# Attention over heads in blocks of two tokens instead of four, in a fused decoder layer on one NeuronCore

## The reference

```python
# 1 attention: over the 16 HEADS of one token, not over tokens
q, k, v = rope(x @ wq.T), rope(x @ wk.T), x @ wv.T      # each (b, s, 16 heads, 16)
weights = softmax(einsum('bshd,bstd->bsht', q, k) / 4)   # per token a 16 by 16 matrix
x = layernorm(x + einsum('bsht,bstd->bshd', weights, v).reshape(b, s, 256) @ wo.T)
# 2 WKV: recurrence over the 128 tokens with k = x, v = ctx
x = layernorm(x + wkv(time_decay, time_first, x, ctx))
# 3 FFN with quantised activations (8 bit, by the row's maximum) and ternary weights
h = silu(bitlinear(x, w1)) * bitlinear(x, w2)            # 704 wide
x = layernorm(x + bitlinear(h, w3))
```

## Time and profile before

| | us |
|---|---|
| median of 3 runs (lowest, highest) | 262.02 (260.38, 263.08) |
| the profiled execution | 262.2 |
| its span, first to last instruction | 260.4 |
| PE busy | 208.2 (80%) |
| DVE busy | 217.7 (84%) |
| ACT busy | 160.9 (62%) |
| POOL busy | 161.5 (62%) |

### The profile page before, as it was taken

The page is one execution under the profiler, slowest core; times in us unless marked ns, Lnnn a source line. Parts: engine busy times, 40 slices in busy tenths (PEclk is TensorE's granted clock), DMA queues, the critical chain, the costliest instruction groups (busy, mean ns, idle before and its releaser), DMA issues.

```text
span 260.4 us, 9989 instructions
## 1 busy us (share of the span) xinstructions
PE 208.2 (80%) x3778; PEld 139.9 (54%) x3778; DVE 217.7 (84%) x544; ACT 160.9 (62%) x329; POOL 161.5 (62%) x336
## 2 busy tenths in 40 slices
PE   1759699989899999999999999999997795625611
PEld 0235457657666666666666666766665662413310
DVE  2534987999999999999999999999999977686331
ACT  2212175446686877777777787777777665655631
POOL 0100007647866869696968778787777787876541
PEclk9986869999999999999999999999999757555665
DMA  6920002102020020212201120203020201000001
GB/s 194 369 66 23 3 1 65 58 7 64 4 64 3 3 83 23 65 29 58 61 26 43 44 71 17 84 3 83 5 63 3 63 3 40 10 13 21 0 20 42
DMA packets 11968, 12.34 MB, mean 47 GB/s; under 512 B 1872, under 2 KB 11152, under 8 KB 11920
## 3 DMA queue, kind: packets, MB, share of 16 engines
q1 hardware_dynamic: 11200, 11.67, 14.5%
q10 hardware_dynamic: 720, 0.03, 0.2%
HBM read 9.60 MB, written 2.10 MB: 45 GB/s over the span
## 4 chain that ended last, share of the span: by engine, by line
PE 50%; DVE 22%; issue 18%; ACT 4%; POOL 3%; DMA 1%; DVEq 1%; POOLq 0%; ACTq 0%
PE ps_qkv L393 13%; PE ps_s L429 9%; PE ps_o L476 5%; PE ps_w L379 4%; DVE amax_h L972 4%; PE ps_c L528 4%; DVE vT L863 3%; PE ps_a L514 3%; DVE qkD L858 3%; PE ps_b L514 3%; DVE gate L965 2%; DVE den_rec L941 2%; PE ps_o L379 2%; DVE wsum L1009 2%; PE ps_o L462 2%
## 5 line engine op out<-in xcount | busy, mean ns | idle before, releaser
L393 PE MATMUL ps_qkv<-wqkv,xT 128*128 128x512 f32 x64 | 35.5, 683 | 1.9 <-DVE qkv_tok L842 1.9
L733 POOL TENSOR_TENSOR var_eps<-mv,eps 128x1 f32<-128x1 f32 x48 | 9.2, 192 | 39.8 <-DVE mv L925 39.3
L745 POOL TENSOR_TENSOR hid<-gate,up_s 128x352 f32<-128x352 f32 x32 | 29.8, 932 | 2.1 <-ACT up_s L628 1.8
L736 POOL TENSOR_TENSOR rstd<-var_eps,minus_half 128x1 f32<-128x1 f32 x48 | 26.4, 551 | 3.8
L941 DVE RECIPROCAL den_rec<-frac 128x256 f32<-128x256 f32 x16 | 27.7, 1733 | 0.0
L429 PE MATMUL ps_s<-qkD 20*64 20x64 f32 x1024 | 23.9, 234 | 3.3 <-PE ps_s L429 3.3
L462 PE MATMUL ps_o<-probs,v_blk 64*32 64x64 f32 x1024 | 21.7, 225 | 4.6 <-DVE res L908 3.6
L577 ACT ACTIVATE qkv_tok<-ps_qkv 128x512 f32<-128x512 f32 x16 | 9.6, 598 | 25.3 <-PE ps_qkv L393 25.3
L387 PE MATMUL ps_qkv<-wqkv,xT 128*128 128x256 f32 x64 | 19.8, 431 | 6.1 <-DMA wqkv<-wqkv_in 5.3
L429 PEld LDWEIGHTS ps_s<-qkD 20*64 20x64 f32 x1024 | 19.8, 143 | 8.1 <-PE ps_s L429 5.1
L660 ACT ACTIVATE hqT<-ps_c 128x768 bf16<-128x768 bf16 x16 | 13.0, 811 | 16.4 <-PE ps_c L521 16.4
(11 more groups left out here) (110 smaller groups left out, 569.5 us busy)
## 6 DMA issues: line engine op xcount, KB each, us to landing
xT<-xT_in SPq DMA_DIRECT2D x16, 128.0 KB, 2.4
x_res<-x_in SPq DMA_DIRECT2D x16, 128.0 KB, 2.7
ctxT<-ctxT_in SPq DMA_DIRECT2D x16, 128.0 KB, 2.4
out<-y_out SPq DMA_DIRECT2D x16, 128.0 KB, 1.7
w_raw<-w_in SPq DMA_DIRECT2D x2, 704.0 KB, 6.7
wqkv<-wqkv_in SPq DMA_DIRECT2D x2, 384.0 KB, 4.2
w_raw<-w_in SPq DMA_DIRECT2D x1, 640.0 KB, 8.6
wo<-wo_in SPq DMA_DIRECT2D x1, 256.0 KB, 4.9
```

The costliest lines, as they stand in the source:

```text
L393: last = mm(ps_kv, xT[k.slot][:, h, :], wqkv[:, h, C:3 * C], start=h == 0, stop=h == 1)
L736: g.tensor_tensor(rstd[i][:], var_eps[i][:], minus_half[:], ALU.pow).then_inc(rstd_done[i], 1)
L745: g.tensor_tensor(hid[:, half * FH:(half + 1) * FH], gate[half][:], up_s[half][:], ALU.mult).then_inc(hid_done[half], 1)
```

## The change

Attention goes in blocks of two tokens. A block's scores are 32 by 32, so that the block of a quad takes just the quad's 32 rows and 32 columns of TensorE (`tile_position`), 16 blocks for each of 4 quads.
- `score`: 64 matmuls of 18 rows by 32 by 32 instead of 32; all scores fit one bank. The pieces' wait within it falls away.
- The maximum is one transposing reduction over 512 columns. POOL `spread_max` multiplies the maxima with a negative diagonal of 32 columns (`neg_diag`), and `shift` is one fp32 matmul of 128 by 512 with a matrix of ones for each quad (`quad_ones`). `max_quads` and the two bf16 parts are gone.
- One exponential over 512 columns instead of two.
- The v blocks come from a second DVE transpose, `block_v`, now on DVE. TensorE's `block_v` and ACT's `copy_v_blocks` are gone.
- `weigh_v`: 64 matmuls of 32 by 32 by 32 in one piece, instead of 32 in two.
- q has a bank of its own. `project_kv` goes ahead of `project_q`, and neither waits for the other.
- The lists of all engines have a new order, with most attention and FFN stages a step earlier on TensorE.

```diff
-BT = 4
+BT = 2
 BLK = BT * HEADS
 MASK_ROWS = HD + BT
+PAIRS = PAD // BT
...
-        neg_eye = sb("neg_eye", [P, 2, BLK], BF16)
+        neg_diag = sb("neg_diag", [P, BLK])
+        quad_sum = sb("quad_sum", [P, QUADS])
+        quad_ones = sb("quad_ones", [P, QUADS, PAD])
...
+        v_blk = [sb(f"v_blk{i}", [P, PAIRS, PAD]) for i in range(2)]
+        row_max = sb("row_max", [P, PAIRS])
+        spread = sb("spread", [P, PAIRS, BLK])
+        probs = sb("probs", [P, PAIRS, BLK])
...
-        ps_qkv = ps("ps_qkv", [P, 512])
-        ps_q = ps_qkv[:, 0:C]
-        ps_kv = ps_qkv[:]
-        ps_s = ps("ps_s", [P, 2, 512])
+        ps_qb = ps("ps_qb", [P, 512])
+        ps_q = ps_qb[:, 0:C]
+        ps_kvb = ps("ps_kvb", [P, 512])
+        ps_kv = ps_kvb[:]
+        ps_s = ps("ps_s", [P, 512])
...
             def project_q(k):
                 wait(pe, ld_xT[k.slot], 16 * (k.pair + 1))
-                wait(pe, v_blocks, k.t)
+                wait(pe, q_copied, k.t)
                 for h in range(HALVES):
                     if k.t == 0:
                         pe.wait_ge(ld_wqkv[h], 16)
...
                 last.then_inc(q_projected, 1)
 
             def project_kv(k):
-                wait(pe, q_copied, k.t + 1)
+                wait(pe, ld_xT[k.slot], 16 * (k.pair + 1))
+                wait(pe, kv_copied, k.t)
                 for h in range(HALVES):
+                    if k.t == 0:
+                        pe.wait_ge(ld_wqkv[h], 16)
                     last = mm(ps_kv, xT[k.slot][:, h, :], wqkv[:, h, C:3 * C], start=h == 0, stop=h == 1)
                 last.then_inc(kv_projected, 1)
 
             def constants():
-                for ready, count in ((ld_ident, 16), (consts, N_CONST), (dve_consts, 3), (ld_wo, 16)):
+                for ready, count in ((ld_ident, 16), (consts, N_CONST), (dve_consts, 4), (ld_wo, 16)):
                     pe.wait_ge(ready, count)
...
 
             def score(k):
                 if k.t == 0:
                     constants()
                 wait(pe, q_dmajor, k.t + 1)
                 wait(pe, k_dmajor, k.t + 1)
...
+                wait(pe, exped, k.t)
+                for y in range(PAIRS):
+                    cols = slice(y * BLK, (y + 1) * BLK)
+                    for g in range(QUADS):
+                        rows = slice(PAD * g, PAD * g + MASK_ROWS)
+                        last = mm(ps_s[PAD * g:PAD * (g + 1), cols], qkD[k.slot][rows, 1, cols],
+                                  qkD[k.slot][rows, 0, cols], start=y == 0, stop=False, skip_group_check=True,
+                                  tile_position=(PAD * g, PAD * g))
                 last.then_inc(scores, 1)
 
             def shift(k):
 
...
+                wait(pe, max_spread, k.t + 1)
+                mm(ps_s[:], quad_ones[:].rearrange("p g x -> p (g x)"), spread[:].rearrange("p y x -> p (y x)"),
+                   start=False, stop=True, skip_group_check=True).then_inc(shifted, 1)
+
+            def weigh_v(k):
+                wait(pe, res_done[0], k.t)
+                wait(pe, v_blocks, k.t + 1)
+                wait(pe, exped, k.t + 1)
+                for y in range(PAIRS):
                     for g in range(QUADS):
...
+                        rows = slice(PAD * g, PAD * (g + 1))
+                        last = mm(ps_o[rows, y * BLK:(y + 1) * BLK], v_blk[k.slot][rows, y, :],
+                                  probs[rows, y, :], start=True, stop=True, tile_position=(PAD * g, PAD * g))
+                last.then_inc(heads_out, 1)
...
+            def exp_scores(k):
+                wait(act, shifted, k.t + 1)
                 wait(act, heads_out, k.t)
-                fn(probs[:, bank, :], ps_s[:, bank, :], ACT.Exp, scale=SCALE).then_inc(exped[bank], 1)
+                fn(probs[:].rearrange("p y x -> p (y x)"), ps_s[:], ACT.Exp, scale=SCALE).then_inc(exped, 1)
...
+            def spread_max(k):
+                if k.t == 0:
+                    pool.wait_ge(dve_consts, 4)
+                wait(pool, maxed, k.t + 1)
+                wait(pool, shifted, k.t)
+                g.tensor_tensor(spread[:], row_max[:].unsqueeze(2).broadcast_to([P, PAIRS, BLK]),
+                                neg_diag[:].unsqueeze(1).broadcast_to([P, PAIRS, BLK]), ALU.mult).then_inc(max_spread, 1)
...
-            v.tensor_scalar(neg_eye[:].rearrange("p a b -> p (a b)"), ident[:], -1.0, None,
-                            ALU.mult).then_inc(dve_consts, 1)
+            v.tensor_reduce(neg_diag[:], ident[:].rearrange("p (g x) -> p x g", g=QUADS), AX.X, ALU.add, negate=True
+                            ).then_inc(dve_consts, 1)
+            v.tensor_reduce(quad_sum[:], ident[:].rearrange("p (g x) -> p g x", g=QUADS), AX.X, ALU.add
+                            ).then_inc(quad_summed, 1)
+            dve.wait_ge(quad_summed, 1)
+            v.tensor_copy(quad_ones[:], quad_sum[:].unsqueeze(2).broadcast_to([P, QUADS, PAD])).then_inc(dve_consts, 1)
...
             def turn_v(k):
                 wait(dve, kv_copied, k.t + 1)
-                wait(dve, v_blocked, k.t)
+                wait(dve, v_blocks, k.t)
                 v.transpose(channel_major(vT[:]), qkv_tok[:, 2]).then_inc(v_turned, 1)
 
-            def max_quads(k):
+            def block_v(k):
+                wait(dve, v_turned, k.t + 1)
+                wait(dve, heads_out, k.t - 1)
+                v.transpose(v_blk[k.slot][:].rearrange("p y x -> p (y x)"), vT[:]).then_inc(v_blocks, 1)
+
+            def max_rows(k):
 
                 wait(dve, scores, k.t + 1)
...
+                wait(dve, max_spread, k.t)
+                v.tensor_reduce(row_max[:], ps_s[:].rearrange("p (y x) -> p y x", x=BLK), AX.X, ALU.max,
+                                apply_transpose=True).then_inc(maxed, 1)
```

More of the change, by code:

```diff
@@ L226, in decoder_layer @@
         dve_consts = sem("dve_consts")
+        quad_summed = sem("quad_summed")
         w3_cleared = sem("w3_cleared")
@@ L414, in score @@
                 wait(pe, k_dmajor, k.t + 1)
[L415 to L429, removed]
-                                      start=(g < 2 and b < 2), stop=False, skip_group_check=True)
-                            if g < 2 and b == 7:
-                                last.then_inc(scored[g], 1)
+                wait(pe, exped, k.t)
@@ L435, in shift @@
             def shift(k):
-                wait(pe, lo_ready, k.t + 1)
-                for bank in range(2):
-                    for s in range(8):
-                        for half in range(2):
-                            o = ps_s[64 * half:64 * half + 64, bank, s * BLK:(s + 1) * BLK]
-                            for part in (max_hi, max_lo):
-                                m = part[:, bank * 8 + s:bank * 8 + s + 1].to_broadcast([P, BLK])
-                                last = mm(o, m, neg_eye[:, half, :], start=False, stop=part is max_lo,
-                                          skip_group_check=True)
-                    last.then_inc(shifted, 1)
@@ L448, in weigh_v @@
-            def weigh_v(k, half):
-                if half == 0:
-                    wait(pe, res_done[0], k.t)
-                    wait(pe, v_blocks, k.t + 1)
-                    for bank in range(2):
-                        wait(pe, exped[bank], k.t + 1)
-                else:
-                    wait(pe, weighed, k.t + 1)
-                rows = slice(64 * half, 64 * half + 64)
-                for jj in range(4):
-                    for g in range(QUADS):
-                        src = (g // 2) * 256 + jj * BLK
-                        dst = (2 * jj + half) * BLK
-                        last = mm(ps_o[PAD * g:PAD * g + PAD, dst:dst + BLK],
-                                  v_blk[k.slot][rows, jj, g, :], probs[rows, g % 2, src:src + BLK],
-                                  start=True, stop=True)
-                last.then_inc(weighed if half == 0 else heads_out, 1)
+                wait(pe, max_spread, k.t + 1)
@@ L1026, in step @@
             def step(at):
-                once(at(0), wkv_tables)
-                on(at(4), mean_var, 1)
+                on(at(4), residual, 1)
+                on(at(5), gate_up, 1)
+                on(at(4), moments, 1)
+                once(at(3), cut_weights, 1)
+                on(at(6), scale_of_out)
+                on(at(4), mean_var, 1)
+                once(at(3), cut_weights, 2)
+                on(at(1), turn_v)
+                once(at(1), wkv_tables)
+                on(at(2), heads_to_tokens)
@@ new lines, in step @@
+                on(at(2), recip_sums)
+                on(at(2), normalise)
+                on(at(6), residual, 2)
+                on(at(5), amax_of_h)
+                on(at(4), amax_of_x)
+                on(at(5), floor_h)
+                on(at(4), floor_x)
+                on(at(5), recip_h)
+                on(at(4), recip_x)
+                on(at(3), scan)
+                on(at(5), scale_of_h)
+                on(at(6), moments, 2)
+                on(at(1), block_v)
+                on(at(6), mean_var, 2)
```

(7 more changed lines are left out.)

153 lines of the change are left out of this document (46 added, 107 removed).

## The result

The changed kernel took 277.19 us (median of 4, 275.52 to 278.33) beside 262.55 for the kernel before (260.38 to 263.11): ratio 1.0569, 95% interval 1.0484 to 1.0653. The forecast was 260.7 with a range of 252 to 271. The time lies above the range, so the forecast was wrong. The profiled execution took 278.33, its span was 276.5.

A forecast was written before the change was run, and what follows sets the result against it. The prediction took VectorE to bound the steady steps, with TensorE and POOL under it. From 262.2 us it added 1.0 for ten steady steps and took off 1.0 for the ramp and 1.5 for the tail: 260.7, range 252 to 271.

The forecast's parts named there:

- Still under VectorE, by 0.6: Steady step: TensorE's summed busy time would be 11.87 us, below VectorE's 12.47, so TensorE would not set the pace.
- 16.3 ns a record: Score and weigh_v on TensorE: the record spacing at which TensorE would pass VectorE and become the bound.
- the ten periods: Steady stretch between the sixth and last tile's scores: ten steps of 12.47 us for 12.37, adding 1.0 us.
- The ramp: Stretch up to the sixth tile's scores: 3 us gained by earlier projections, 2 us lost to rounding of FFN weights' sums.
- the tail: Stretch after the last tile's scores: -3.8 us from moving `down`, +2.4 from spreading and longer score and weighing, net -1.5.
- The second rival: Score and weigh_v: issuing costs more on 32 by 32 tiles, TensorE becomes the bound, 265 to 285 us; chance 0.13.
- 14.0 ns a record: Score and weigh_v on TensorE: 128 records start 14.0 ns apart, set by issuing, so each block takes 1.99 us.
- the block at the low clock: Old weighing block in the tail: 24.7 ns a record, less than twice 14.0 at half clock, a sign for issuing.
- VectorE: VectorE's steady step: 0.25 us gained by the new instructions, 0.35 lost to dependent neighbours, so 12.47 us for 12.37.
- The reduction: VectorE's new transposing reduction of 512 elements a row: 0.63 us a tile from start to start.
- POOL: POOL's steady step: `spread_max` adds 1.19 us to 9.64, so busy 10.83 us of 12.4, not the bound.
- its loop: Third rival: the loop from VectorE through POOL's in-order list sets the step, up to 13.56 us, 264 to 272; chance 0.20.

The follow-up runs named there:

- run 7: Changed kernel in its own order, half the instructions in score and weigh_v over the same columns (computes other scores and sums than the reference): 259.65 us in one execution.
- 11: The same half-instruction edit of the changed kernel's score and weigh_v, timed again against the kernel before: 261.16 us in ten executions, ratio 0.9959.
- run 5: Changed kernel with TensorE's list reordered: project_kv ahead of turn_attn, score behind both: 265.4 us, ratio 1.016 to the kernel before.
- run 1: Changed kernel with TensorE's list alone altered: score moved away from weigh_v, behind the next step's project_kv: 275.6 us, ratio 1.0362 to the kernel before.
- 9: Changed kernel with score and weigh_v each split in two halves on TensorE, other work between, project_q inside weigh_v: 311.09 us, ratio 1.1873 to the kernel before.
- 8: Changed kernel with project_kv ahead of turn_attn, score behind both, and project_q ahead of turn_xq too: 265.75 us, ratio 1.0111 to the kernel before.

## Why the prediction was wrong

**The step that failed** is the comparison of TensorE with VectorE: "Still under VectorE, by 0.6", and behind it 16.3 ns a record as the point from which the change costs. It took TensorE's order as a sum of busy times. I had the number of records and their price, but not where they stand: 256 instructions in 1.3 us, 3.2 us from 256 others. The limit that this hits isn't a time for each record but one for each 256 instructions, and it shows mostly where two such pieces stand near each other; the mean of a step, about 600 in 12.55 us, is well under it. The term for the supply of instructions was nowhere in the sum. In the trace the ten periods from the sixth tile's scores (81.91) to the last's (216.25) take 134.3 us and not 123.6, +10.8 where I had +1.0, with three steps of 13.6, 15.2 and 15.2 in them. The ramp, to 81.91 and not 77.30, costs 4.6 where I had a gain of 1.0, and the tail 0.7 where I had a gain of 1.5. Together that is the span's 276.5 against 260.4.

**The second rival** (TensorE bound by issuing, 265 to 285) had the engine and the size right, the mechanism wrong. It asked for over 16.3 ns a record and PE over 98%. Neither is there: records start (1.29 - 0.20) / 127 = 8.6 ns apart, and PE is busy for 85% of the long step. It had a chance of 0.13, and that 277 falls in its range is luck.

**14.0 ns a record** was an end of the range: 8.6 was measured, so columns count, not issuing alone. From the block at the low clock I had read too much for issuing. TensorE came to 10.85, not 11.87. The rule of the Trainium skill, "TensorE: Matmul & The Clock Gate", Part 1, that starts are never closer than about 25 ns, was doubted in the prediction by its rows; the mean of 8.6 ns contradicts it for these tiles.

**VectorE** was right in sum: 12.55 for 12.47. The reduction took 0.60 from start to start (0.63), `block_v` 0.62 (0.61), and VectorE was over 98% busy in an undisturbed step.

**POOL** was right: 10.7 for 10.83, and its loop costs nothing, the undisturbed step is VectorE's.

**Ramp and tail.** Without the stops (run 7, span 257.9) the first scores start at 11.6, the sixth at 70.35, the last at 196.79; before, 18.08, 77.30 and 200.88. So the ramp gives 6.9 us back where I took 1.0, ten periods cost 2.9 (12.64 on average, with the last ones longer, where I took 12.47), and the tail costs 1.6 where I took a gain of 1.5. The sum is -2.5; I had -1.5. In the changed kernel the first scores are nearly as early (12.29), the sixth start at 81.91: the stops begin in the ramp, at 21.4.

**The forecast without the stops** is measured by runs 7 and 11, 259.65 and 261.16 for 260.7. The count of the engines' work in a step was right. That the total came so near is partly luck: the ramp gained 5.9 us more than I had, the ten periods lost 1.9 more and the tail 3.1 more.

## What to carry to other kernels

Count instructions, not only busy time: where small tiles make a block of some 256 instructions in a microsecond or two, look how long ago the last such block was, and set them apart by other work. Some 5 us from start to start ended most stops in run 5, but not all; fewer instructions ended them all in the steady stretch. Look for "issue" in the middle of a block, in steps of a fixed number of records, and for the packets of the instruction queue beside them. And before moving a block, ask what it covered and who reads what moves with it: of the reorderings here, those that opened a hole ahead of the projections or put a step behind its reader (runs 1 and 9) lost again what they won. None of the versions that compute what the reference does beat the kernel before; the best (runs 5 and 8) are 1.1 to 1.6% slower.

## What of the hardware was unexpected

- TensorE's instructions come in packets of 16 KB, 256 instructions each. In the changed kernel a piece of short ones took 3.1 to 3.9 us at 13 of 17 stops and 4.1 to 4.9 at four; two of these four lie at loads 1108 and 1991, as in several other runs, and why is open. In other runs single stops came up to 11.5 us after the entry of the piece before.
- One fp32 matmul record with its weight load on a 32 by 32 tile goes every 8.6 ns on average over a block of 128 on the four diagonal tiles.
- A stop of 1.6 us (the changed kernel), or two holes of 0.8 and 1.0 us close together (the profiled execution of run 1), was followed by kv at the lower clock: 3.6 us instead of 1.88. Holes of 1.2 us (run 5) and of 0.9 us (the changed kernel's undisturbed steps) were not.
